# New half-step positions for projections, values, bulk loads and the last feed-forward stage in a two-layer gated cross-attention kernel

## The chip, the cores and the metric

The kernel runs on one core of one Trainium2 chip. The metric is the device time of one execution in microseconds (us). Engines are named as in the profile: PE is TensorE (matmul), DVE is VectorE, ACT is ScalarE, POOL is GpSimd, and SP is SyncE, whose queue issues nearly all DMA transfers. Each engine works through its own instructions in order and waits on semaphores for the others.

## What is computed

The input `x` has 4 sequences of 512 tokens with 256 features. Two layers follow each other. Each adds a gated cross-attention to `x`, and then a gated feed-forward part. The first layer's feed-forward part is a mixture of 8 experts, of which each token uses 2. The second layer's is two linear layers with ternary weights and 8-bit activations, with a gelu between them.

```
x = x + tanh(g_xattn[0]) * attention0(layernorm(x), ctx, ctx)
x = x + tanh(g_ffn[0])   * top2_experts(layernorm(x))
x = x + tanh(g_xattn[1]) * attention1(layernorm(x), ctx, ctx)
x = x + tanh(g_ffn[1])   * bitlinear(gelu(bitlinear(layernorm(x), w1)), w2)

attention: q, k, v = projections; 16 heads of 16 features
  softmax(q @ k.T / 4) @ v, then an output projection
```

## The kernel before, in words

**Phases and half steps.** There are 8 phases, one for each layer and sequence: phases 0 to 3 are the attention of layer 0, phases 4 to 7 that of layer 1. A phase has 16 groups of four heads by 128 keys, and each group is done in two halves, so that a phase has 32 half steps, called slots here (0 to 31). In each slot PE does two score matmuls `S` into the three banks of `psS` (L747), which DVE reduces to row maxima (L1166). It then does two transposed score matmuls `T` into `psT` (L761), which ACT turns into exponentials with one instruction of 128x1024 (L986). `S` runs 12 slots ahead of `T`, because the maxima have to be written back as extra rows of the queries first: POOL splits them in two parts (L643, L646), PE transposes them (L784), ACT copies them to `mt` (L1002), and SP writes them with four DMAs into `qs` (L526). In every odd slot PE also multiplies the exponentials of an earlier group with the values, `PV` (L775, eight matmuls in the trace). Every eighth slot (2, 10, 18, 26) has four transpositions of the attention's output, `NT` (L792), and every eighth (4, 12, 20, 28) one of the maxima, `MT` (L784).

**The other work.** All else is hung into slots by a table written by hand, `work_table`. `put(p, s, item)` puts an item behind the `S`, `T` and `PV` of slot `s` of phase `p`. `pair` puts an item for both halves of the features. Every engine walks through the same table and does its part of each item in that order. The items that matter here are:

- `SPLIT` (`K` or `Q`, phase, half): a projection, on PE four matmuls of 128x512 in the trace (L702) into a bank of `psX`. ACT then reads the bank twice (L933, L934), POOL forms the low part (L569), and SP writes both parts to DRAM (L498 to L502). They come back into `qs` and `ks` with `RELOAD` (L516).
- `VV`: the values, eight matmuls (L722) into `psX`, read by DVE (L1120).
- `LD`: bulk loads by SP (L444): `w1` and `w2` are 1 MB each into `hh`, `x3` 512 KB, `k1` 256 KB. `ABS` (L1131) and `QUANT` (L1151, L1154) are DVE's sums and ternary weights from `w1` and `w2`.
- `LNC` and `LNN`: the normalisation, eight small POOL operations (L586 to L605) and ACT's scaling (L943). `ST` is its statistics on DVE (L1095), `XT` the transposition (L733) with ACT's copy (L956), `BIAS` an addition on POOL (L616), `MH` a copy of expert weights on ACT (L971).
- In phases 5 to 7, and behind the last phase for the last sequence: `XQ`, `XI`, `XB` (scaling on POOL L652, rounding on ACT L1016, transposition L851 and ACT's copy L1026), `F1` (the first linear layer, L874, and ACT's gelu L1037 over 128x1024), `HQ` (DVE L1328 to L1338, POOL L658), `HS` (ACT L1048), `HT` (PE L884, ACT L1062), `F2` (PE L892, DVE L1348), `XOUT` (the output, SP L533). There are four tiles of 128 tokens each.

**Banks.** The small results share the two banks of `psX` in turn, and an item waits until the one before it in the same bank has been read. The gelu inputs `F1` of tiles 0 and 2 are written to the two banks of `psT`, those of tiles 1 and 3 to both banks of `psX`. ACT needs another function table for gelu than for the exponential, so the trace has a table load on either side of a block of gelus.

**Start and end.** The 12 slots ahead of phase 0 are slots 20 to 31 of a phase named `lead`, in which only `S` runs. In front of them the first two sequences are normalised and projected.

The functions of the kernel that the change touches are these.

## Time and profile before

| | before |
|---|---|
| device time, three runs | 811.45 us median (808.52 to 812.57) |
| profiled execution, its device time | 810.76 us |
| its span in the trace | 809.0 us |
| mean granted TensorE clock | 0.919 of full |
| busy PE, DVE, ACT, POOL | 709.5, 529.0, 448.7, 168.1 us |

The device time of the profiled execution is 1.8 us above its span. Slot starts are read off the exponentials (L986), of which there is one in each slot: the first starts at 53.5 us, the last phase's last one at 759.1 us. The phases start at 53.5, 145.1, 239.2, 328.5, 417.3, 506.2, 600.8 and 685.5 us, and slots 8 and 16 of phase 0 at 76.9 and 99.6 us.

### The profile page before, as it was taken

To read this page: it belongs to the slowest core of one execution; us is meant where nothing else is said; L and a number is where in the kernel's file an instruction comes from. 1 tells how busy PE (TensorE), PEld (TensorE's weight loads), DVE (VectorE), ACT (ScalarE), POOL (GpSimd) and SP (SyncE) were. 2 spreads that over 40 slices of the span, in tenths; PEclk is the share of its full clock that TensorE was granted. 3 is DMA by queue.
4 is the path that set the end of the run, shared out by engine and by line. 5 is a ranking of instruction groups with operands and counts; after the bars stand their busy time and mean duration, and the time that the engine had idled before them with its cause. 6 is when DMAs were issued, how large, how long until landed. Compare 5 with 4: busy or idle time off the path is not lost.

```text
span 809.0 us, 10145 instructions
## 1 busy us (share of the span) xinstructions
PE 709.5 (88%) x3554; PEld 333.6 (41%) x3554; DVE 529.0 (65%) x1138; ACT 448.7 (55%) x572; POOL 168.1 (21%) x302
## 2 busy tenths in 40 slices
...
DMA packets 39922, 66.74 MB, mean 82 GB/s; under 512 B 6080, under 2 KB 14784, under 8 KB 39616
## 3 DMA queue, kind: packets, MB, share of 16 engines
...
## 4 chain that ended last, share of the span: by engine, by line
PE 64%; ACT 12%; DVE 11%; issue 6%; POOL 5%; DMA 1%; SPq 0%; POOLq 0%; DVEq 0%; ACTq 0%
PE psO L775 14%; PE psS L747 7%; PE psT L761 7%; PE psX L702 7%; PE psX L836 5%; ACT pt L986 5%; DVE mx L1166 4%; PE psX L812 4%; PE psX L837 4%; PE psX L838 3%; PE psX L722 3%; PE psX L892 2%; DVE xs L1297 2%; PE psX L733 2%; ACT parts L934 1%
## 5 line engine op out<-in xcount | busy, mean ns | idle before, releaser
L1166 DVE TENSOR_REDUCE mx<-psS 128x1 f32<-128x512 f32 x512 | 324.7, 681 | 121.6 <-PE psS L747 121.3
L986 ACT ACTIVATE pt<-psT 128x1024 f32<-128x1024 f32 x256 | 261.6, 1022 | 225.1 <-PE psT L761 222.8
L747 PE MATMUL psS<-ks,qs 48*128 48x512 f32 x512 | 155.4, 519 | 16.6 <-DVE mx L1166 16.0
L775 PE MATMUL psO<-pt,vg 128*32 128x512 f32 x1024 | 148.6, 655 | 0.1
L761 PE MATMUL psT<-qs,ks 50*128 50x512 f32 x512 | 120.6, 444 | 24.1 <-ACT pt L986 22.2
L747 PEld LDWEIGHTS psS<-ks,qs 48*128 48x128 f32 x512 | 61.1, 194 | 128.2 <-issue 70.6
L1297 DVE SCALAR_TENSOR_TENSOR xs<-psX,coef,xs 128x256 f32<-128x256 f32 x128 | 61.8, 483 | 32.3 <-PE psX L838 29.2
L569 POOL TENSOR_TENSOR parts<-qf,parts 128x512 fp32r<-128x512 f32 x32 | 40.8, 1274 | 190.8 <-ACT parts L934 190.8
L761 PEld LDWEIGHTS psT<-qs,ks 50*128 50x128 f32 x512 | 53.3, 196 | 46.8 <-ACT pt L986 44.2
L836 PE MATMUL psX<-moeh,xh 128*128 128x512 f32 x128 | 57.5, 449 | 4.4 <-DVE xs L1297 4.4
L837 PE MATMUL psX<-moel,xh 128*128 128x512 f32 x128 | 51.0, 398 | 0.0
L838 PE MATMUL psX<-moeh,xl 128*128 128x512 f32 x128 | 50.3, 393 | 0.0
L702 PE MATMUL psX<-ctxb,wk 128*128 128x512 f32 x64 | 39.6, 754 | 7.6 <-DMA wk<-in_Wk 7.6
L836 PEld LDWEIGHTS psX<-moeh,xh 128*128 128x128 f32 x128 | 24.1, 189 | 43.6 <-DVE xs L1297 22.5
L643 POOL CAST mp<-mx 128x16 fp32r<-128x16 f32 x32 | 6.7, 208 | 169.6 <-DVE mx L1166 169.3
L943 ACT ACTIVATE xn<-xs,lnw 128x256 f32<-128x256 f32 x60 | 31.8, 590 | 15.8 <-POOL lnw L605 15.7
L658 POOL TENSOR_SCALAR hh<-hh,am 128x1024 f32<-128x1024 f32 x16 | 17.9, 1120 | 107.1 <-DVE am L1338 107.1
L775 PEld LDWEIGHTS psO<-pt,vg 128*32 128x32 f32 x1024 | 20.6, 110 | 43.3 <-issue 42.2
L702 PE MATMUL psX<-xnt,wq 128*128 128x512 f32 x64 | 35.0, 676 | 2.0 <-ACT xnt L956 1.6
L722 PE MATMUL psX<-wv,ctxb 128*128 128x256 f32 x128 | 32.8, 402 | 0.0
L812 PE MATMUL psX<-wo,ont 128*128 128x256 f32 x128 | 31.6, 391 | 0.8 <-ACT ont L979 0.8
L1095 DVE BATCH_NORM_STATS2 st<-xs 128x6 f32<-128x256 f32 x64 | 26.4, 413 | 7.3 <-DMA xs<-in_x 6.6
(128 smaller groups left out, 745.9 us busy)
## 6 DMA issues: line engine op xcount, KB each, us to landing
ks<-kd SPq DMA_DIRECT2D x64, 192.0 KB, 3.7
qs<-qd SPq DMA_DIRECT2D x64, 192.0 KB, 4.6
kd<-parts SPq DMA_DIRECT2D x16, 512.0 KB, 2.8
qd<-parts SPq DMA_DIRECT2D x16, 512.0 KB, 2.7
...
ctxb<-in_ctxT SPq DMA_DIRECT2D x7, 512.0 KB, 3.4
xs<-in_x SPq DMA_DIRECT2D x4, 512.0 KB, 6.8
```

The lines of the kernel that those rows point to most:

```text
L702: i = mm(o, w[:, k, c * P:(c + 1) * P], src[:, k, :], start=k == 0, stop=k == NC - 1)
L722: i = mm(o[:, t * D:(t + 1) * D], ctxb[:, p % 2, k, (2 * half + t) * P:(2 * half + t + 1) * P], wv[l][:, k, :], start=k == 0, stop=k == NC ...
L747: mm(psS[:, i % 3, :], qs[at:at + KR, 2 * g + a, k * P:(k + 1) * P], ks[at:at + KR, 2 * g + a, :], start=True, stop=True).then_inc(pe_s, 1)
L761: i = mm(psT[:, r, :], ks[at:at + KR + MP, 2 * g + half, k * P:(k + 1) * P], qs[at:at + KR + MP, 2 * g + half, :], start=True, stop=True)
L775: i = mm(psO[32 * j:32 * j + 32, :], vg[:, p % 2, k, g * GH + j, :], pt[:, s % RING, j, :], start=k == 0, stop=k == NT - 1, tile_position= ...
L812: i = mm(o[:, t * D:(t + 1) * D], ont[:, k, tt * P:(tt + 1) * P], wo[l][:, k, :], start=k == 0, stop=k == NC - 1)
L836: mm(o, xh[:, k, tok], moeh[:, k, at], start=k == 0, stop=False)
L837: mm(o, xh[:, k, tok], moel[:, k, at], start=False, stop=False)
L838: i = mm(o, xl[:, k, tok], moeh[:, k, at], start=False, stop=k == NC - 1)
L986: a(pt[:, G % RING, 2 * half:2 * half + 2, :], psT[:], ACT.Exp, scale=SCALE).then_inc(a_exp, 1)
L1166: v.tensor_reduce(mx[:, w // GH % 2, r, col:col + 1], psS[:, i % 3, :], AX.X, ALU.max).then_inc(v_max, 1)
L1297: v.scalar_tensor_tensor(out=xs[:, b, t, :], in0=o[:, k * D:(k + 1) * D], scalar=coef[:, t, e:e + 1], in1=xs[:, b, t, :], op0=ALU.mult, op ...
```

## The change

Nothing that is computed changes. The items have other places, `F1` of tiles 1 and 3 has other banks, and the waits follow the banks.

- The two projections `Q` of phase 1, until now ahead of the first exponential, stand in slots 0 and 4 of phase 0. All projections of phases 0 and 1 stand in even slots (14 in phase 0, where there were 10, and 2 in phase 1, where there were 4). In phases 5 and 6 the two `K` projections move from slots 1 and 13 to 2 and 12.
- The values of phase 1 move from slots 13 and 15 of phase 0 to 8 and 14.
- The loads `x3`, `w1`, `w2` and `k1` are issued in slots 0, 1, 3 and 4 of phase 0. They stood ahead of the first exponential.
- `ABS` moves from slots 3 and 5 to 9 and 11, the `QUANT` items to the even slots 14 to 28.
- `F1` of tiles 1 and 3 goes to the first two banks of `psS`. It waits for the maxima, and the next `S` waits for the gelus. In phases 5 and 6 the values stand behind `F1` of tiles 1 and 2; they stood ahead of tiles 0 and 1.
- Behind the last phase all four `F1` are done first, then all `HQ`, then `HS`, `HT` and `F2` in turn.

```diff
-    put(lead, 26, ("LD", ("w1",)))
-    put(lead, 28, ("LD", ("w2",)))
-    put(lead, 29, ("SPLIT", ("Q", 1, 1)))
...
-    pair(0, 23, "SPLIT", "K", 4, step=2)
-    pair(0, 27, "SPLIT", "K", 5, step=2)
...
+    put(0, 0, ("SPLIT", ("Q", 1, 0)), ("LD", ("x3",)), ("BIAS", (1, 0)))
+    put(0, 1, ("LD", ("w1",)))
...
+    pair(0, 20, "SPLIT", "K", 4, step=2)
+    pair(0, 24, "SPLIT", "K", 5, step=2)
...
-                put(p, 1, ("SPLIT", ("K", p + 1, 0)))
-                put(p, 13, ("SPLIT", ("K", p + 1, 1)))
+                put(p, 2, ("SPLIT", ("K", p + 1, 0)))
+                put(p, 12, ("SPLIT", ("K", p + 1, 1)))
...
-                if p < NP - 1 and t < 2:
-                    put(p, 16, ("VV", (p + 1, t)))
                 put(p, 16, ("F1", (t,)))
+                if p < NP - 1 and t in (1, 2):
+                    put(p, 16, ("VV", (p + 1, t - 1)))
...
-    out += [("LD", (one,)) for one in ("bo", "x2", "k1", "x3")]
+    out += [("LD", (one,)) for one in ("bo", "x2")]
...
-    out += [("SPLIT", ("Q", 1, 0))]
...
(scores S)
+                    if due(a_f1, n("F1")):
+                        pe.wait_ge(a_f1, n("F1"))
                     mm(psS[:, i % 3, :], qs[at:at + KR, 2 * g + a, k * P:(k + 1) * P], ks[at:at + KR, 2 * g + a, :],
...
(gelu input F1)
                 if t % 2:
-                    for b in range(2):
-                        if due(*last[b]):
-                            pe.wait_ge(*last[b])
-                        last[b] = (a_f1, i + 1)
-                    o = psX
+                    if due(v_max, n("S", 2)):
+                        pe.wait_ge(v_max, n("S", 2))
+                    o = psS
                 else:
                     if due(a_exp, n("T")):
                         pe.wait_ge(a_exp, n("T"))
-                    if due(a_f1, i - 1):
-                        pe.wait_ge(a_f1, i - 1)
                     o = psT
+                if due(a_f1, i - 1):
+                    pe.wait_ge(a_f1, i - 1)
                 if due(a_xb, n("XB")):
                     pe.wait_ge(a_xb, n("XB"))
```

Three places on PE show what the table does. The first is PE's order from the transposition of the second normalised sequence (L733, after the change L738) to the first exponentials' scores. `psS` are the scores for the maxima, `psT` the transposed ones, `mp` the maxima, and `psX<-xnt,wq` a projection of queries. Before:

```order
L733 MATMUL psX<-identf,xn 128x128 x8
L702 MATMUL psX<-xnt,wq 128x512 x2
L747 MATMUL psS<-ks,qs 128x512 x18
L784 MATMUL psX<-identf,mp 32x128
L747 MATMUL psS<-ks,qs 128x512 x2
L702 MATMUL psX<-xnt,wq 128x512 x2
L747 MATMUL psS<-ks,qs 128x512 x6
L761 MATMUL psT<-qs,ks 128x512 x2
L747 MATMUL psS<-ks,qs 128x512 x2
```

After:

```order
L738 MATMUL psX<-identf,xn 128x128 x8
L754 MATMUL psS<-ks,qs 128x512 x18
L791 MATMUL psX<-identf,mp 32x128
L754 MATMUL psS<-ks,qs 128x512 x8
L768 MATMUL psT<-qs,ks 128x512 x2
L707 MATMUL psX<-xnt,wq 128x512 x2
L754 MATMUL psS<-ks,qs 128x512 x2
```

The two projections have left the stretch ahead of the first `psT`; the first of them now stands right behind it.

The second place is PE in slots 24 to 28 of phase 0, where the projections of keys for later phases stand (`psX<-ctxb,wk`). `psO` is `PV`, and `identf,osb` is `NT`. Before:

```order
L747 MATMUL psS<-ks,qs 128x512 x2
L761 MATMUL psT<-qs,ks 128x512 x2
L747 MATMUL psS<-ks,qs 128x512 x2
L761 MATMUL psT<-qs,ks 128x512 x2
L775 MATMUL psO<-pt,vg 32x512 x4
L702 MATMUL psX<-ctxb,wk 128x512 x2
L747 MATMUL psS<-ks,qs 128x512 x2
L761 MATMUL psT<-qs,ks 128x512 x2
L792 MATMUL psX<-identf,osb 128x128 x4
```

After:

```order
L754 MATMUL psS<-ks,qs 128x512 x2
L768 MATMUL psT<-qs,ks 128x512 x2
L707 MATMUL psX<-ctxb,wk 128x512 x2
L754 MATMUL psS<-ks,qs 128x512 x2
L768 MATMUL psT<-qs,ks 128x512 x2
L782 MATMUL psO<-pt,vg 32x512 x4
L754 MATMUL psS<-ks,qs 128x512 x2
L768 MATMUL psT<-qs,ks 128x512 x2
L799 MATMUL psX<-identf,osb 128x128 x4
L707 MATMUL psX<-ctxb,wk 128x512 x2
```

The projection stood behind `PV` in the odd slot; it now stands directly behind `T` of the even slot, and in one even slot of four behind `NT`.

The third place is PE behind the last phase. `w1q,xit` is `F1`, `identb,hq` is `HT`, `w2q,hqt` is `F2`, and `identb,xi` is `XB`. Before:

```order
L851 MATMUL psX<-identb,xi 128x128 x4
L874 MATMUL psT<-w1q,xit 128x512 x4
L874 MATMUL psX<-w1q,xit 128x512 x4
L851 MATMUL psX<-identb,xi 128x128 x4
L874 MATMUL psT<-w1q,xit 128x512 x4
L884 MATMUL psX<-identb,hq 128x128 x8
L874 MATMUL psX<-w1q,xit 128x512 x4
L892 MATMUL psX<-w2q,hqt 128x256 x8
L884 MATMUL psX<-identb,hq 128x128 x8
L892 MATMUL psX<-w2q,hqt 128x256 x8
L884 MATMUL psX<-identb,hq 128x128 x8
```

After:

```order
L858 MATMUL psX<-identb,xi 128x128 x4
L879 MATMUL psT<-w1q,xit 128x512 x4
L858 MATMUL psX<-identb,xi 128x128 x4
L879 MATMUL psS<-w1q,xit 128x512 x4
L879 MATMUL psT<-w1q,xit 128x512 x4
L879 MATMUL psS<-w1q,xit 128x512 x4
L889 MATMUL psX<-identb,hq 128x128 x16
L897 MATMUL psX<-w2q,hqt 128x256 x8
L889 MATMUL psX<-identb,hq 128x128 x8
```

The fourth `F1` stood behind the first `HT`, which needs the first tile's whole way through `HQ` and `HS`; all four now stand together ahead of it.

## Rows read from the trace of the kernel before

**Rows 1.** The page: shares of the chain that ended last, by engine.
```profile
PE 64%; ACT 12%; DVE 11%; issue 6%; POOL 5%; DMA 1%; SPq 0%; POOLq 0%; DVEq 0%; ACTq 0%
```

**Rows 2.** Windows: stretch, us, PE, PEld, DVE, ACT, POOL busy, PEclk, DMA, GB/s.
```profile
0.00:53.50 53.50, 38.01 (x87) 17.68 (x87) 24.03 (x50) 13.72 (x23) 25.32 (x40) 0.81 0.87 256
53.50:76.90 23.40, 19.78 (x70) 6.75 (x69) 15.51 (x26) 13.12 (x19) 7.87 (x14) 0.71 0.47 167
...
99.60:145.10 45.50, 39.65 (x171) 14.98 (x170) 28.41 (x50) 26.97 (x37) 12.21 (x11) 0.92 0.49 151
...
761.20:809.00 47.80, 23.82 (x120) 14.14 (x116) 16.01 (x46) 20.53 (x25) 10.53 (x24) 0.70 0.03 11
```

**Rows 3.** Timeline ahead of the first exponential: start, us, engine, instruction, idle before.
```profile
29.12 3.75 PE L702 MATMUL psX<-xnt,wq 128*128 128x512 f32 x4 [0.78 <-ACT xnt L956]
...
32.80 0.93 PE L747 MATMUL psS<-ks,qs 48*128 48x512 f32 x3
...
45.07 2.84 SPq L526 DMA_DIRECT2D qs<-mt  x4
...
45.40 3.78 PE L702 MATMUL psX<-xnt,wq 128*128 128x512 f32 x4
...
52.97 0.50 PE L761 MATMUL psT<-qs,ks 50*128 50x512 f32 x2 [0.59 <-DMA qs<-mt]
```

**Rows 4.** DMA issues, median us to landing: 25:26.8 us, then 150:400 us.
```profile
qs<-qd SPq DMA_DIRECT2D x2, 192.0 KB, 3.7
...
kd<-parts SPq DMA_DIRECT2D x4, 512.0 KB, 2.8
```

**Rows 5.** Timeline of slots 23 to 25 of phase 0.
```profile
120.64 1.02 ACT L986 ACTIVATE pt<-psT 128x1024 f32<-128x1024 f32 x1 [0.60 <-PE psT L761]
...
121.52 1.98 PE L702 MATMUL psX<-ctxb,wk 128*128 128x512 f32 x4
...
124.70 1.02 ACT L986 ACTIVATE pt<-psT 128x1024 f32<-128x1024 f32 x1
...
126.31 1.02 ACT L986 ACTIVATE pt<-psT 128x1024 f32<-128x1024 f32 x1 [0.59 <-PE psT L761]
```

**Rows 6.** A group of DVE: `ABS`; busy us, mean ns, idle before.
```profile
L1131 DVE TENSOR_REDUCE wsum<-hh 128x1 f32<-128x2048 f32 x2 | 4.5, 2264 | 0.0
```

**Rows 7.** Timeline of slots 16 and 17 of phase 1.
```profile
191.34 1.98 PE L702 MATMUL psX<-ctxb,wk 128*128 128x512 f32 x4
...
191.45 1.02 ACT L986 ACTIVATE pt<-psT 128x1024 f32<-128x1024 f32 x1 [4.08 <-PE psT L761]
...
194.51 1.02 ACT L986 ACTIVATE pt<-psT 128x1024 f32<-128x1024 f32 x1
```

**Rows 8.** Timeline of slots 13 and 14 of phase 6.
```profile
631.74 1.02 ACT L986 ACTIVATE pt<-psT 128x1024 f32<-128x1024 f32 x1 [0.74 <-PE psT L761]
...
638.46 1.02 ACT L986 ACTIVATE pt<-psT 128x1024 f32<-128x1024 f32 x1
```

**Rows 9.** Timeline of slot 16 of phase 5: second gelu and next exponential.
```profile
562.18 1.11 ACT L1037 ACTIVATE hh<-psX,am 128x1024 f32<-128x1024 f32 x1 [2.51 <-PE psX L874]
...
566.85 1.02 ACT L986 ACTIVATE pt<-psT 128x1024 f32<-128x1024 f32 x1
```

**Rows 10.** Timeline behind the last phase.
```profile
781.21 1.11 ACT L1037 ACTIVATE hh<-psX,am 128x1024 f32<-128x1024 f32 x1 [0.35 <-PE psX L874]
...
784.15 1.88 PE L874 MATMUL psT<-w1q,xit 128*128 128x512 bf16 x4 [0.69 <-ACT xit L1026]
...
792.35 1.11 ACT L1037 ACTIVATE hh<-psX,am 128x1024 f32<-128x1024 f32 x1 [1.98 <-PE psX L874]
...
806.38 0.48 DVE L1348 SCALAR_TENSOR_TENSOR xs<-psX,am,xs 128x256 f32<-128x256 f32 x1 [2.61 <-PE psX L892]
```

**Rows 11.** Groups in 778:809 us: busy us, mean ns, idle before.
```profile
L1048 ACT ACTIVATE hq<-hh,negm 128x1024 bf16<-128x1024 f32 x4 | 4.6, 1138 | 0.0
L1062 ACT ACTIVATE hqt<-psX 128x1024 bf16<-128x1024 bf16 x4 | 4.1, 1023 | 6.7 <-PE psX L884 6.7
```

More of the change, by code:

```diff
@@ L111, in work_table @@
-    put(0, 5, ("LNN", (2, 0, 2)), ("SPLIT", ("K", 1, 1)), ("ABS", (1,)))
-    put(0, 6, ("LNN", (2, 2, 4)))
-    pair(0, 7, "XT")
-    put(0, 8, ("BIAS", (2, 0)))
-    put(0, 9, ("SPLIT", ("Q", 2, 0)), ("LD", ("moe1",)))
-    put(0, 10, ("WS", ()))
-    put(0, 11, ("SPLIT", ("Q", 2, 1)))
-    put(0, 13, ("VV", (1, 0)), ("LNC", (3, 0, NT)))
-    put(0, 15, ("VV", (1, 1)), ("LNN", (3, 0, 2)))
-    put(0, 16, ("LNN", (3, 2, 4)))
-    pair(0, 17, "XT")
-    put(0, 18, ("BIAS", (3, 0)))
-    pair(0, 19, "SPLIT", "Q", 3, step=2)
@@ L124, in work_table @@
-    pair(0, 23, "SPLIT", "K", 4, step=2)
-    put(0, 22, ("LD", ("v1",)))
-    put(0, 26, ("LD", ("q1",)), ("CTX", (2,)))
-    pair(0, 27, "SPLIT", "K", 5, step=2)
-    put(0, 30, ("CTX", (3,)))
-    for q, s in enumerate((11, 13, 15, 19, 21, 23, 25, 27)):
-        put(0, s, ("QUANT", (q // 4, q % 4)))
-    pair(1, 1, "SPLIT", "K", 2, step=3)
-    pair(1, 6, "SPLIT", "K", 3, step=10)
+        st(0, 5 + t, 3, t)
+    put(0, 0, ("SPLIT", ("Q", 1, 0)), ("LD", ("x3",)), ("BIAS", (1, 0)))
+    put(0, 1, ("LD", ("w1",)))
@@ new lines, in work_table @@
+    put(0, 2, ("SPLIT", ("K", 1, 0)))
+    put(0, 3, ("LNC", (2, 0, NT)), ("LD", ("w2",)))
+    put(0, 4, ("SPLIT", ("Q", 1, 1)), ("LD", ("k1",)))
+    put(0, 5, ("LNN", (2, 0, 2)))
+    put(0, 6, ("SPLIT", ("K", 1, 1)), ("LNN", (2, 2, 4)))
+    pair(0, 7, "XT", step=2)
+    put(0, 8, ("VV", (1, 0)), ("BIAS", (2, 0)), ("LD", ("moe0",)))
+    put(0, 9, ("ABS", (0,)), ("LNC", (3, 0, NT)))
+    pair(0, 10, "SPLIT", "Q", 2, step=2)
+    put(0, 11, ("ABS", (1,)), ("LNN", (3, 0, 2)))
+    put(0, 12, ("LNN", (3, 2, 4)), ("LD", ("moe1",)))
@@ new lines, in work_table @@
+    pair(0, 13, "XT", step=2)
+    put(0, 13, ("WS", ()))
+    put(0, 14, ("VV", (1, 1)), ("BIAS", (3, 0)))
+    pair(0, 16, "SPLIT", "Q", 3, step=2)
+    put(0, 18, ("LD", ("o",)))
+    pair(0, 20, "SPLIT", "K", 4, step=2)
+    put(0, 23, ("CTX", (2,)))
+    pair(0, 24, "SPLIT", "K", 5, step=2)
+    put(0, 25, ("LD", ("rt",)))
+    put(0, 27, ("CTX", (3,)))
+    pair(0, 28, "SPLIT", "K", 2, step=2)
+    put(0, 29, ("LD", ("v1",)))
+    for q in range(8):
+        put(0, 14 + 2 * q, ("QUANT", (q // 4, q % 4)))
@@ L133, in work_table @@
+    pair(1, 0, "SPLIT", "K", 3, step=2)
+    put(1, 4, ("LD", ("q1",)))
     for i in range(MOE_PARTS):
```

25 lines of the change are left out of this document (13 added, 12 removed).

## The prediction

> **What bounds the kernel now.** I read the shares of the chain first, then the windows by stage, then the timelines of the places that the change touches. PE has 64% of the chain that ended last [rows 1], but that is a mean over stages. The windows [rows 2] tell four of them apart. Ahead of the first exponential (53.5 us) PE is granted 0.81 of its clock and the DMA engines are busy at 0.87. The first 8 slots of phase 0 take 23.4 us at a granted clock of 0.71. Slots 16 to 31 take 45.5 us at 0.92. The last 47.8 us have PE busy for half of the time, at 0.70.
>
> Inside phase 0 the chain goes back and forth. An exponential starts, PE does `PV` and then the projection, ACT has to read the projection twice, and the next exponential stands behind those reads. In slot 23 the exponential starts at 120.64, the projection only at 121.52, and the next exponential at 124.70: 4.06 us [rows 5]. The even slot behind it, with no projection, takes 126.31 - 124.70 = 1.61 us. Of the 4.06 us, 0.88 is `PV`, which nobody awaits so soon. So what counts is what stands between `T` and ACT's reads. That is what the change touches.
>
> **Start: -5.5 us.** A projection of 3.75 us (29.12 to 32.8) stands ahead of the first `S` at 32.80 [rows 3]. Without it `S` waits for `qs`, whose two writes are issued from 25 us on and land 3.7 us later [rows 4], so at about 29.5: 3.3 us earlier. The way from there to the DMAs of the maxima (45.07) keeps its length, 12.3 us, since DVE's maxima set it. They start at 41.8 instead of 45.07, and the last of the four is issued 2.1 us later, at 43.9. Before, `T` waited for them until 52.97, 5 us behind the last issue, with `w1` in the queue ahead of them. With the bulk loads gone I take the 2.8 us of a write in a calm stretch [rows 4], which gives 46.7. Ten maxima between are DVE's at some 0.6 us each, 41.8 - 1 + 6.2 = 47.0. The second projection (45.40, 3.78 us at the low clock) is gone as well. So `T` starts near 47.3 instead of 52.97; I take -5.5. The bounds are -3.3 (the landing stays as it was) and -6.2.
>
> The trace shows the maxima's writes landing only behind `w1`. The Trainium skill states as a rule that each DMA engine takes the descriptors of one issuing engine's ring in order (DMA: Bandwidth & Descriptors, section on queues, rings and completion order), and by that rule the trace agrees. By it the wait isn't lost but moved: the bulk now stands ahead of phase 0's own transfers. That is the second rival below.
>
> **Phases 0 and 1: -6 us.** The price of a projection is what its slot takes above 1.61 us. In an odd slot that is 4.06 - 1.61 = 2.45 us [rows 5]. For an even slot there is one at full clock before: slot 16 of phase 1, 191.45 to 194.51, 3.06 us, with the projection starting at 191.34, right at the exponential [rows 7]. Its price is 1.45 us. `PV` then falls into the next slot, beneath ACT's reads and the exponential.
> - Before: 10 odd in phase 0, 1 odd and 3 even in phase 1: 11 x 2.45 + 3 x 1.45 = 31.3 us. After: 16 even, 23.2 us. This has the two `Q` that come out of the start in it. -8.1 us.
> - In slots 0 to 7 (clock 0.71) two projections ran at the low clock, at 3.78 instead of 1.98 us [rows 3, 5]. I expect one to stay so, the one in slot 0, and the denser PE to be granted the full clock behind it: -1.8 us.
> - The two `VV` no longer stand behind `PV`: 2 x 0.88 = -1.8 us.
> - Against it: `NT` stands ahead of a projection in slots 10, 18 and 26, `MT` in 4, 12, 20 and 28. Both are shorter than `PV`'s 0.88; I take 0.5 and 0.3, together +2.7 us.
> - `ABS` blocks DVE for 2.26 us twice [rows 6]. In slots 3 and 5 that lay beside slow projections; in 9 and 11 there is none, and two of DVE's maxima per slot are late. `S` has three banks, so a part is absorbed: +1.5 us each, +3 us.
> - POOL (1.3 us a projection), SP and the DMAs have a pair of slots, 4.7 us, for each: hidden.
>
> The sum is -6.0. Its bounds are +2 (an even slot is worth nothing, `NT`, `MT` and `ABS` cost in full, the clock gives nothing) and -11 (they cost nothing).
>
> **Phases 5 and 6: -8 us.** `K` from slot 1 to 2: 1.0 us each, -2. `K` from 13 to 12: slot 13 of phase 6 takes 638.46 - 631.74 = 6.72 us [rows 8], with `PV` and the projection at the low clock. In slot 12 the projection runs on PE beneath ACT's four scalings (slot 11) and the exponential, so that only ACT's two reads remain. The bounds are 0 and -3.8; I take -2 each, -4. In phase 5 POOL did the low part of the slot 1 projection ahead of the normalisation of slot 1, for which ACT waits in slot 3: -1. The gelus: in phase 5 ACT sat 2.51 us ahead of the second [rows 9], since `F1` of tile 1 waited for `VV` in `psX`. But both `VV` now stand between tile 1 and tile 3, and PE's work in the block stays 6.9 us, so most of the gap comes back ahead of the third and fourth: I take -0.6 each, -1.2 (bounds 0 and -2.5 each).
>
> The block has a new wait: `S` of slot 17 waits for the fourth gelu, and behind it on PE stand `T` and `PV`; ACT's next exponential waits for `T`. ACT loads its table meanwhile (the exponential at 566.85 [rows 9] is 1.3 us behind the last gelu), and `S` plus `T` need 0.8 us at full clock, so it costs nothing; at the low clock it would cost 0.3 us.
>
> **End: -8 us.** Before, the second gelu starts at 781.21, then ACT turns to `XI` and `XB` of the second half, PE's third `F1` follows at 784.15, and the fourth gelu starts at 792.35, behind `HS` and `HT` of tile 0 [rows 10]. After, `XI` is done ahead of the first gelu and `XB`'s copy behind it, at 781.5. `F1` of tile 1 waits for that copy, which isn't needed for its tile: gelu 1 at 782.4 (full clock, half of the 1.88 us) or 783.3, so 1 to 2 us later than before. The others follow at 1.05 us or, at the low clock, at 1.7 us. The fourth ends at 785.8 to 787.8 instead of 793.5. Then ACT has 4 `HS` of 1.14 and 4 `HT` copies of 1.02 [rows 11], 8.6 us. The last `HS` waits for DVE's and POOL's part of tile 3, which is due near 790.5 and ready in time. The last transposition (1.0), the last `F2` (1.0 to 1.9) and DVE's 0.48 come behind: 796.9 to 800.6. Before, the last DVE operation ends at 806.86 [rows 10]. So -6.3 to -10; I take -8.
>
> **Sum.** -5.5 - 6 - 8.2 - 8 = -27.7. The profiled execution took 810.76 us, of which 809.0 are its span; that gives 783.1. The median of the runs shown is 0.7 us above the profiled one. I predict 783 us.
>
> **Rivals.**
> - *PE is the bound and the half step doesn't matter.* For it: 64% of the chain, and PE's total work is unchanged. Against it: 3.06 against 4.06 us in the rows. Then phases 0, 1, 5 and 6 keep their length and only start and end remain: 810.8 - 13.5 = 797 us. Chance 0.13.
> - *The bulk stands in the way of phase 0.* `x3`, `w1` and `w2` (2.5 MB) and two projections' parts (1.5 MB) are issued ahead of the second group's maxima (slot 4), which are due for `T` in slot 8. 4.0 MB at the start's 256 GB/s [rows 2] are 16 us from about 54, so 70, against slot 8 near 70 to 72. A few us of wait there, some at `ST` of `x3` (DVE's maxima queue behind it) and at later reloads make +8: 791 us. Chance 0.15. This is what the ring order of the Trainium skill's DMA page would do here.
> - *The clock stays low: slower.* With a projection in every second slot at the low clock, a pair of slots has 8.7 us of PE work instead of 4.7: the projection +1.8 [rows 3, 5], and as much again for scores and `PV`, so +4 us a pair. Seven such pairs of the 16 in phase 0 eat the 28 us, eight make it 815. For it: slots 0 to 7 had 0.71. Against it: slots 16 to 31 had 0.92 with the same work less dense. Chance 0.03. The Trainium skill (TensorE: Matmul & The Clock Gate, part on the HAM clock gate) has it that idleness lowers the clock and activity releases it, which speaks against this rival.
>
> **Numbers.** The forecast has 0.69, with a range of its own of 775 to 791. The range for all is 773 to 797: below it are the far bounds of start, slots and end together, above it half of the first rival and the third. About 0.5% is what a measurement can tell here. Faster by more: 0.95; within: 0.02; slower: 0.03.
>
> **What would show it.** First exponential near 48 us. Slots 20 to 31 of phase 0 in pairs of 3.1 and 1.6 us. Phases 2, 3 and 4 at 89 us as before. Slots 12 to 15 of phases 5 and 6 shorter by 2 us. Four gelus without a gap behind the last phase and the fourth ending by 788. I am wrong if the even slots take 4 us, if `T` of slot 8 waits for `mt`, or if PE's clock in phase 0 is under 0.8.

## The result, and the profile after

The changed kernel takes 768.44 us (median of 4 runs, 766.51 to 770.32) against 809.99 us before (4 runs, 806.96 to 812.57). The ratio is 0.9488, with a 95% interval of 0.9442 to 0.9534. I had predicted 783.0 us with a range of 773 to 797: the direction was right, the gain of 41.5 us is one and a half times the forecast one of 27.7, and the time lies below the range. A ratio leaves out the runs that lie more than 1.5% above the fastest run of their kernel.

The profiled execution has a span of 764.7 us against 809.0. Cut at the first exponential of each phase, and for the end where the last exponential stops (760.2 us before, 724.9 after; [rows 2] cuts at 761.2), the windows are these (us, busy us of PE, PEld, DVE, ACT, POOL with instructions, PEclk, DMA share, GB/s), for the start, phases 0, 1, 5, 6 and 7, and the end:

```profile
0.00:46.90 46.90, 30.68 (x78) 15.62 (x78) 23.62 (x50) 11.06 (x19) 21.08 (x37) 0.81 0.76 216
46.90:132.10 85.20, 78.39 (x355) 30.30 (x356) 63.15 (x112) 56.98 (x80) 31.13 (x41) 0.97 0.71 231
132.10:222.10 90.00, 84.27 (x439) 42.19 (x440) 65.80 (x150) 47.08 (x64) 19.29 (x28) 0.98 0.28 72
488.60:572.40 83.80, 75.00 (x434) 34.32 (x435) 59.51 (x119) 62.04 (x77) 20.14 (x37) 0.98 0.29 84
572.40:650.50 78.10, 68.47 (x412) 31.57 (x412) 57.07 (x114) 56.80 (x67) 12.93 (x26) 1.00 0.26 69
650.50:724.90 74.40, 62.59 (x358) 25.79 (x358) 41.19 (x87) 54.35 (x61) 10.05 (x22) 0.91 0.07 17
724.90:764.70 39.80, 22.15 (x123) 13.46 (x124) 15.92 (x46) 20.34 (x26) 10.58 (x24) 0.79 0.05 16
```

The kernel before, cut in the same way, for phases 5 and 6:

```profile
506.20:600.80 94.60, 84.10 (x435) 36.72 (x435) 59.70 (x119) 62.40 (x77) 20.07 (x37) 0.87 0.27 74
600.80:685.50 84.70, 74.59 (x413) 32.83 (x412) 57.32 (x114) 57.04 (x67) 12.95 (x26) 0.92 0.24 64
```

The reader is to compare PE in phase 5: 435 matmuls before and 434 after, but 84.10 us busy before and 75.00 after, at a granted clock of 0.87 and 0.98. Phases 5 and 6 together lose 15.2 us of PE's busy time with the same work. The clock has two levels here, 2.4 GHz (granted 1.0) and 1.2 GHz (0.5), so a window of 94.60 us at 0.87 holds 2 x 0.13 x 94.6 = 25 us at the low one. Read from the clock's own records it is 23.9 us. By stage (us of length, and behind the stroke the us of it at 1.2 GHz; 2 to 4 are three phases together, of some 89 us each):

| | start | 0 | 1 | 2 to 4 | 5 | 6 | 7 | end | span |
|---|---|---|---|---|---|---|---|---|---|
| before | 53.5/21 | 91.5/21 | 94.1/7 | 267.0/3 | 94.6/24 | 84.7/14 | 74.7/14 | 48.8/28 | 809.0 |
| after | 46.9/18 | 85.1/6 | 90.0/3 | 266.6/0 | 83.8/3 | 78.1/0 | 74.4/14 | 39.8/17 | 764.7 |
| difference | -6.6 | -6.4 | -4.1 | -0.5 | -10.8 | -6.6 | -0.3 | -9.0 | -44.3 |
| predicted | -5.5 | -6, both | | 0 | -8.2, both | | 0 | -8 | -27.7 |

The whole program had 131 us at the low clock before and 61 us after. These are one execution of each kernel, but the sign isn't luck: of the 33 runs of before beside the experiments none has a mean granted clock above 0.937, and of the 8 runs of the changed kernel none has one below 0.953. The chain that ended last has changed with it; to [rows 1] answers:

```profile
PE 56%; DVE 14%; ACT 12%; issue 9%; POOL 6%; DMA 2%; SPq 0%; POOLq 0%; DVEq 0%; ACTq 0%
```

**Start.** The timeline of after, up to the first exponential, which answers to [rows 3] (start, us, engine, instruction, idle before and who ended it):

```profile
29.61 1.22 PE L754 MATMUL psS<-ks,qs 48*128 48x512 f32 x3 [2.11 <-DMA qs<-qd]
...
42.03 2.84 SPq L531 DMA_DIRECT2D qs<-mt  x4
...
46.06 0.80 PE L768 MATMUL psT<-qs,ks 50*128 50x512 f32 x2
46.79 1.22 PE L707 MATMUL psX<-xnt,wq 128*128 128x512 f32 x1
46.90 1.02 ACT L991 ACTIVATE pt<-psT 128x1024 f32<-128x1024 f32 x1 [4.90 <-PE psT L768]
```

`S` starts at 29.61 where I had said 29.5, the four writes are issued at 42.03 (41.8), and `T` at 46.06 no longer waits for them: its line has no bracket.

**Phase 0.** Slots 24 and 25 of after, with a projection in the even one. This answers to [rows 5] and [rows 7]:

```profile
111.94 1.98 PE L707 MATMUL psX<-ctxb,wk 128*128 128x512 f32 x4
112.05 1.02 ACT L991 ACTIVATE pt<-psT 128x1024 f32<-128x1024 f32 x1 [0.69 <-PE psT L768]
...
113.96 0.69 ACT L938 ACTIVATE qf<-psX,bkc 128x512 f32<-128x512 f32 x1 [0.89 <-PE psX L707]
...
114.55 0.68 ACT L939 ACTIVATE parts<-psX,bkc 128x512 fp32r<-128x512 f32 x1
115.12 1.02 ACT L991 ACTIVATE pt<-psT 128x1024 f32<-128x1024 f32 x1
...
116.73 1.02 ACT L991 ACTIVATE pt<-psT 128x1024 f32<-128x1024 f32 x1
```

The even slot takes 115.12 - 112.05 = 3.07 us, the odd one 1.61: the pair takes 4.68 where it took 5.67 before.

**Phase 6.** Slots 12 and 13 of after, beside [rows 8]:

```profile
599.50 1.88 PE L707 MATMUL psX<-ctxb,wk 128*128 128x512 f32 x4
600.63 1.00 ACT L991 ACTIVATE pt<-psT 128x1024 f32<-128x1024 f32 x1
...
602.83 1.00 ACT L991 ACTIVATE pt<-psT 128x1024 f32<-128x1024 f32 x1
...
604.42 1.03 ACT L991 ACTIVATE pt<-psT 128x1024 f32<-128x1024 f32 x1 [0.59 <-PE psT L768]
```

The projection lies beneath ACT's scalings and the exponential, and takes 1.88 us instead of 3.78. Slots 12 and 13 take 2.2 and 1.6 us, where they took 1.9 and 6.7.

**End.** The timeline of after from the rounding of the second half (L1021) to the fourth gelu (L1042), which answers to [rows 10]:

```profile
740.45 0.72 ACT L1021 ACTIVATE xi<-xn,negm 128x512 bf16<-128x512 f32 x1
...
743.00 1.49 PE L879 MATMUL psT<-w1q,xit 128*128 128x512 bf16 x3 [1.09 <-ACT xit L1031]
...
744.52 1.11 ACT L1042 ACTIVATE hh<-psT,am 128x1024 f32<-128x1024 f32 x1 [0.81 <-PE psT L879]
745.53 0.59 ACT L1031 ACTIVATE xit<-psX 128x512 bf16<-128x512 bf16 x1
...
746.27 1.86 PE L879 MATMUL psS<-w1q,xit 128*128 128x512 bf16 x4 [1.36 <-ACT xit L1031]
...
748.17 1.11 ACT L1042 ACTIVATE hh<-psS,am 128x1024 f32<-128x1024 f32 x1 [2.05 <-PE psS L879]
...
750.52 1.11 ACT L1042 ACTIVATE hh<-psS,am 128x1024 f32<-128x1024 f32 x1
```

The fourth gelu ends 26.7 us behind the last exponential (724.9); it was 33.3 us before. The second gelu still waits 2.05 us, for an `F1` that waited for the second half's copy and then ran at the low clock.

### The profile page after: what moved, and what is told of

Its sections match the earlier page's. It is cut to its first block, busy times and chain, and to the rows that moved or that the text cites. A ratio compares the mean times of both kernels' runs of the same rounds, so it can differ in the third digit from the quotient of the medians.

```text
span 764.7 us, 10140 instructions
## 1 busy us (share of the span) xinstructions
PE 676.7 (88%) x3550; PEld 323.6 (42%) x3554; DVE 530.5 (69%) x1138; ACT 446.8 (58%) x572; POOL 167.0 (22%) x302
## 4 chain that ended last, share of the span: by engine, by line
PE 56%; DVE 14%; ACT 12%; issue 9%; POOL 6%; DMA 2%; SPq 0%; POOLq 0%; DVEq 0%; ACTq 0%
PE psO L782 10%; PE psS L754 7%; PE psX L707 7%; DVE mx L1171 6%; PE psT L768 6%; PE psX L843 5%; PE psX L819 4%; ACT pt L991 4%; PE psX L844 4%; PE psX L845 4%; PE psX L727 3%; ACT qf L938 2%; DVE xs L1302 2%; POOL parts L574 2%; ACT parts L939 2%
## 5 line engine op out<-in xcount | busy, mean ns | idle before, releaser
L1171 DVE TENSOR_REDUCE mx<-psS 128x1 f32<-128x512 f32 x512 | 325.1, 681 | 87.4 <-PE psS L754 86.1
L754 PE MATMUL psS<-ks,qs 48*128 48x512 f32 x512 | 153.8, 516 | 18.9 <-DVE mx L1171 13.2
L782 PE MATMUL psO<-pt,vg 128*32 128x512 f32 x1024 | 140.4, 621 | 0.1
L768 PE MATMUL psT<-qs,ks 50*128 50x512 f32 x512 | 118.2, 431 | 9.6 <-ACT pt L991 8.2
L843 PEld LDWEIGHTS psX<-moeh,xh 128*128 128x128 f32 x128 | 23.9, 187 | 43.9 <-DVE xs L1302 23.8
L707 PE MATMUL psX<-ctxb,wk 128*128 128x512 f32 x64 | 34.4, 667 | 7.7 <-DMA wk<-in_Wk 7.7
L707 PE MATMUL psX<-xnt,wq 128*128 128x512 f32 x64 | 32.2, 630 | 1.3 <-ACT xnt L961 0.8
L1125 DVE TENSOR_TENSOR vg<-psX,bvb 128x512 f32<-128x512 f32 x16 | 11.0, 691 | 29.1 <-PE psX L727 29.1
```

What stands on the lines that cost most here:

```text
L707: i = mm(o, w[:, k, c * P:(c + 1) * P], src[:, k, :], start=k == 0, stop=k == NC - 1)
L754: mm(psS[:, i % 3, :], qs[at:at + KR, 2 * g + a, k * P:(k + 1) * P], ks[at:at + KR, 2 * g + a, :], start=True, stop=True).then_inc(pe_s, 1)
L768: i = mm(psT[:, r, :], ks[at:at + KR + MP, 2 * g + half, k * P:(k + 1) * P], qs[at:at + KR + MP, 2 * g + half, :], start=True, stop=True)
L782: i = mm(psO[32 * j:32 * j + 32, :], vg[:, p % 2, k, g * GH + j, :], pt[:, s % RING, j, :], start=k == 0, stop=k == NT - 1, tile_position= ...
L843: mm(o, xh[:, k, tok], moeh[:, k, at], start=k == 0, stop=False)
L1171: v.tensor_reduce(mx[:, w // GH % 2, r, col:col + 1], psS[:, i % 3, :], AX.X, ALU.max).then_inc(v_max, 1)
```

## The experiments

Each took its place beside runs of the kernel before on the same chip. x1 to x4 shared one chip (before: 807.75 us, median of 7), y1 to y3 and z1 another (807.6, 19 runs), the last four a third (802.62, 7 runs). Lengths of stages are those of each kernel's profiled execution. The intervals of the ratios reach 0.4 to 1.2% to either side, so the lengths of the stages, and not the whole times, tell the theories apart.

**x1_k56: only the projections of phases 5 and 6, in the kernel before.**

```diff
-                put(p, 1, ("SPLIT", ("K", p + 1, 0)))
-                put(p, 13, ("SPLIT", ("K", p + 1, 1)))
+                put(p, 2, ("SPLIT", ("K", p + 1, 0)))
+                put(p, 12, ("SPLIT", ("K", p + 1, 1)))
```

> The kernel before with one part of the change: in phases 5 and 6 the two key projections stand in slots 2 and 12 instead of 1 and 13. Theory CLOCK (the low-clock stretches of phases 5 and 6, 23.9 and 13.7 us of them before and 3.4 and 0 after, came from PE standing idle ahead of the projections, and go with the move): phases 5 and 6 shorten together by 12 us or more, their granted clock rises from 0.87 and 0.92 to over 0.96, ratio near 0.98. Theory PRICE (only the slots that hold the projections get shorter, as the prediction had it): 6 to 7 us, low-clock time nearly as before, ratio near 0.992.

Measured: 797.21 us, ratio 0.987 (0.9782 to 0.9959), 10.5 us less than before. Phase 5 takes 87.9 us (-6.7) and phase 6 78.8 (-5.9). The windows:

```profile
503.10:591.00 87.90, 79.73 (x436) 35.34 (x435) 59.74 (x120) 62.04 (x76) 20.06 (x37) 0.92 0.28 82
591.00:669.80 78.80, 70.08 (x413) 31.41 (x412) 57.13 (x113) 56.80 (x66) 12.88 (x26) 0.98 0.26 68
```

With two lines moved by one slot the two phases are 12.6 us shorter, against the 7 us that I had for them. Of the 12.6, 2.4 are slot 5 of phase 5, which is shorter in x2_end too, without this edit. PE's busy time in the two falls by 8.9 us with the same instructions, as the granted clock goes from 0.87 and 0.92 to 0.92 and 0.98. Slots 12 to 15 take 10.7 and 8.4 us instead of 12.7 each. Neither theory was met in full: the 12 us of CLOCK came, but the granted clock of phase 5 stayed at 0.92 (10.2 us at the low clock from 559.7 us on), and the ratio lies between the two that were named.

**x2_end: only the gelus' banks, the values between them and the order of the end, in the kernel before.**

```diff
-                if p < NP - 1 and t < 2:
-                    put(p, 16, ("VV", (p + 1, t)))
                 put(p, 16, ("F1", (t,)))
+                if p < NP - 1 and t in (1, 2):
+                    put(p, 16, ("VV", (p + 1, t - 1)))
...
+    put(NP, 5, ("F1", (0,)), ("XB", (2, 4)), ("F1", (1,)), ("F1", (2,)), ("F1", (3,)))
...
-                a(hh[:, t, :], (psX if t % 2 else psT)[:].rearrange("p a b -> p (a b)"), ACT.Gelu,
+                a(hh[:, t, :], (psS if t % 2 else psT)[:, 0:2, :].rearrange("p a b -> p (a b)"), ACT.Gelu,
```

> The kernel before with the new banks for the gelu inputs, the values behind the inputs of tiles 1 and 2, and the new order of the end. Both theories: the end takes 7 to 9 us less; slot 16 of phases 5 and 6 0.2 to 0.6 us less each; phases 0 to 4 unchanged. CLOCK adds that phases 5 and 6 keep their low-clock stretches ahead of slot 16, so that no more than 2 us come from them: ratio near 0.988.

Measured: 795.88 us, ratio 0.988 (0.9783 to 0.9977), with runs from 784 to 809 us, of which the profiled one is the fastest. The end takes 40.1 us, 8.7 less than before. Slot 16 of phases 5 and 6 goes from 11.1 and 10.8 to 10.6 us, and slots 17 to 21 of phase 5 from 13.3 to 10.2. In x1_k56, which left the block alone, these take 13.3 as before. So the gelus themselves gave 0.6 us, and the slots behind them 3.1 in phase 5, where before had 10.2 us at the low clock from 569.2 on and this kernel has none. Slots 12 to 15 stayed at 12.7 and 13.4 us, so what was gained there belongs to `K`. What was gained behind slot 16 goes with the block's new order, but it is the low clock that went and not work that got shorter. In the eight cases with the old order (phases 5 and 6 of before, x1_k56, y1_fill6 and y3_lnc) slots 17 to 21 take between 13.3 us, with 10.2 at the low clock, and 9.5 us, with none. The new order takes 10.2 in every profile, with no low clock, and at the full clock the old one is the shorter of the two.

Two parts of the expectation missed. Phases 5 and 6 are 6.6 us shorter, not 2 at most. And phases 0 and 1, where this kernel has the same instructions as before, took 88.2 and 91.0 us instead of 91.5 and 94.1, with 13 us at the low clock instead of 27. One execution of the same instructions differs from another by 6.4 us there.

**x3_odd: the projections and values of phases 0 and 1 one slot later, in the changed kernel.**

```diff
-    pair(0, 16, "SPLIT", "Q", 3, step=2)
-    pair(0, 20, "SPLIT", "K", 4, step=2)
-    pair(0, 24, "SPLIT", "K", 5, step=2)
+    pair(0, 17, "SPLIT", "Q", 3, step=2)
+    pair(0, 21, "SPLIT", "K", 4, step=2)
+    pair(0, 25, "SPLIT", "K", 5, step=2)
...
```

> The changed kernel with the 16 projections and the 2 values of phases 0 and 1 one slot later, in the odd slots, all else as changed. Theory PRICE: 16 projections at 1.0 us and 2 values at 0.9 us more, less some 2 us because the transpositions of the attention output and of the maxima no longer stand ahead of them: phases 0 and 1 longer by 14 to 16 us. Rival (PE is the bound in these phases, the half step doesn't matter, and the gain there came from the clock and from moving the sums of the weights): longer by less than 5 us.

Measured: 791.62 us, ratio 0.974 (0.9623 to 0.9858). Phases 0 and 1 take 107.3 and 92.2 us, together 24.3 more than in the changed kernel and more than the 14 to 16 expected. The window of phase 0:

```profile
47.00:154.30 107.30, 92.15 (x356) 35.13 (x355) 65.36 (x112) 57.29 (x80) 27.75 (x39) 0.88 0.57 180
```

In slots 16 to 31 the pairs stand at 4.1 + 1.6 us again. With the one disturbed slot (25, 5.7 us) counted at 4.1, these sixteen take 45.5 us against 39.9, 0.7 us for each of the eight projections; the prediction had 1.0, less 0.17 for `NT` and `MT`. That gives 11 us for 16. Of the 24.3, 7.1 lie in slots 16 to 31, 2.2 in phase 1 and 15.0 in slots 0 to 15, 60.2 us against 45.2, with 23 us at the low clock there instead of 6. The half step has nearly its forecast price where the clock is full, and more time at the low clock goes with it. How much of the 15.0 us is the one and how much the other this run can't tell, since the sums of the weights on DVE (L1136) stand beside projections here.

**x4_loads: the bulk loads back ahead of the first exponential, in the changed kernel.**

```diff
+    put(lead, 26, ("LD", ("w1",)))
+    put(lead, 28, ("LD", ("w2",)))
...
-    put(0, 1, ("LD", ("w1",)))
```

`w2`, `k1` and `x3` go back in the same way.

> The changed kernel with the four bulk loads back ahead of the first exponential, the projections staying in phase 0. If the wait of the first T for the maxima's writes came from the loads ahead of them in the queue, the first exponential is later by 3 to 5 us and phase 0 keeps its length. Rival (the 6.5 us of the start came from the two projections alone): first exponential later by less than 1 us. If the bulk costs phase 0 something in the changed kernel, phase 0 gets shorter here by what it costs; I expect less than 1.5 us.

Measured: 772.43 us, ratio 0.9579 (0.9503 to 0.9654). The start takes 50.6 us (+3.7), phase 0 86.1 (+1.0). The timeline:

```profile
38.01 0.43 SPq L450 DMA_DIRECT2D hh<-in_w  x1
...
41.90 2.84 SPq L532 DMA_DIRECT2D qs<-mt  x4
...
44.78 0.44 SPq L450 DMA_DIRECT2D hh<-in_w  x1
...
49.81 0.80 PE L769 MATMUL psT<-qs,ks 50*128 50x512 f32 x2 [3.55 <-DMA qs<-mt]
```

The first `hh<-in_w` is `w1`, issued ahead of the maxima's writes, and the second is `w2`, issued behind them. The chain that ended last has the fourth write from its issue to its landing:

```profile
44.10 5.66 DMA qs<-mt
```

`T` waits 3.55 us for the writes of the maxima again. `w1` took 10.9 us to land, to 48.9, and the fourth write landed at 49.8, ahead of `w2` (7.1 us, to 51.9): the load that stood ahead of the writes held them up. Of the 6.6 us at the start, 3.7 are the loads' and the other 2.9 the two projections'. Phase 0 isn't shorter for having its loads done early, so the bulk was not in its way. One reservation: the start scatters too, 46.7 to 47.1 us in six other profiles with the changed start and 49.7 in z2_q12, where `T` doesn't wait for the writes.

**y1_fill6: five matmuls that nobody reads behind slot 11 and five behind slot 12, in phases 5 and 6, in the kernel before.** Nothing else is moved, and nothing is left out.

```diff
+    for p in (5, 6):
+        put(p, 11, ("FILL", (5,)))
+        put(p, 12, ("FILL", (5,)))
...
+                for _ in range(count):
+                    mm(psX[:, b, :], identb[:], w1q[:, 0, 0:S], start=True, stop=True)
```

> The kernel before with ten idle matmuls of 128x512 in each of phases 5 and 6 (five in slot 11, five in slot 12, their result is never read), nothing moved. They add 2.2 us of PE work per phase at full clock, in a stretch in which PE stands idle. Theory CLOCK: the low clock that comes in slots 12 and 13 (6.8 us of it in phase 6, the projection at 3.78 us) is gone or shorter, and slots 12 to 15 of phases 5 and 6, 12.6 us each before, shrink to about 11 although work was added. Theory PRICE (it is the order of the work alone): they stay at 12.6 us or grow by up to 2.2.

Measured: 800.11 us (10 runs), ratio 0.9921 (0.9876 to 0.9965). Work was added and the kernel got 0.8% faster. Phase 5 takes 88.9 us (-5.7), phase 6 82.0 (-2.7); slots 12 to 15 take 9.9 and 10.1 us instead of 12.7 each, with no low clock. In phase 6 slots 10 and 11 grew by 0.9 us, with 3.4 us at the low clock from 620.2 us on. Slot 13 of phase 6, with the added matmuls (L905) ahead of it:

```profile
624.93 1.24 PE L905 MATMUL psX<-w1q,identb 128*128 128x512 bf16 x5
...
626.89 1.02 ACT L998 ACTIVATE pt<-psT 128x1024 f32<-128x1024 f32 x1 [0.80 <-PE psT L765]
627.77 1.99 PE L706 MATMUL psX<-ctxb,wk 128*128 128x512 f32 x4
...
629.79 0.69 ACT L945 ACTIVATE qf<-psX,bkc 128x512 f32<-128x512 f32 x1 [1.88 <-PE psX L706]
...
630.95 1.02 ACT L998 ACTIVATE pt<-psT 128x1024 f32<-128x1024 f32 x1
```

The slot takes 4.06 us, as any odd slot at full clock, instead of 6.72: the projection 1.99 instead of 3.78. The kernel before has PE waiting ahead of this slot, and the slow projection in it:

```profile
630.90 0.79 PE L761 MATMUL psT<-qs,ks 50*128 50x512 f32 x2 [1.59 <-ACT pt L986]
...
633.48 3.78 PE L702 MATMUL psX<-ctxb,wk 128*128 128x512 f32 x4
```

It waited 1.59 us, behind ACT's four scalings, and the low clock began at 630.6, within that wait. With PE kept busy it didn't. This isn't one lucky execution: with `K` in slot 13 and nothing added, slots 12 to 15 have 5.9 to 9.5 us at the low clock in all six cases (phases 5 and 6 of before, x2_end and y3_lnc), and none in the two of y1_fill6. The Trainium skill (TensorE: Matmul & The Clock Gate, part on the HAM clock gate) says that idleness drops the clock and activity raises it; this pair of runs agrees, 3.78 against 1.99 us.

**y3_lnc: the normalisation ahead of the projection in slot 1 of phase 5 alone, in the kernel before.**

```diff
-                put(p, 1, ("SPLIT", ("K", p + 1, 0)))
+                if p != B + 1:
+                    put(p, 1, ("SPLIT", ("K", p + 1, 0)))
...
             put(p, 1, ("LNC", (p - 2, 0, NT)))
+            if p == B + 1:
+                put(p, 1, ("SPLIT", ("K", p + 1, 0)))
```

> The kernel before with one thing in phase 5: the normalisation's small POOL operations of slot 1 stand ahead of the projection of slot 1 instead of behind it, so that POOL doesn't do the projection's low part first. PRICE: slot 3 of phase 5 falls from 4.2 to about 3.0 us, nothing else: -1.2 us. CLOCK: PE's idle stretch ahead of the low clock of slots 3 to 5 goes, slot 5 falls from 4.0 to 1.6 us as well: phase 5 shorter by 3 us or more.

Measured: 799.0 us (10 runs), ratio 0.9919 (0.9871 to 0.9967). Phase 5 takes 88.8 us (-5.8). Slot 3 of phase 5, before:

```profile
514.09 1.02 ACT L986 ACTIVATE pt<-psT 128x1024 f32<-128x1024 f32 x1 [0.60 <-PE psT L761]
...
516.85 1.09 ACT L943 ACTIVATE xn<-xs,lnw 128x256 f32<-128x256 f32 x2 [1.75 <-POOL lnw L605]
...
518.33 1.01 ACT L986 ACTIVATE pt<-psT 128x1024 f32<-128x1024 f32 x1
```

and in y3_lnc:

```profile
507.56 1.02 ACT L989 ACTIVATE pt<-psT 128x1024 f32<-128x1024 f32 x1 [0.60 <-PE psT L764]
...
508.48 1.08 ACT L946 ACTIVATE xn<-xs,lnw 128x256 f32<-128x256 f32 x2
...
509.94 1.02 ACT L989 ACTIVATE pt<-psT 128x1024 f32<-128x1024 f32 x1
```

ACT's wait of 1.75 us for POOL is gone and the slot takes 2.38 instead of 4.24 us. Slot 5 went from 4.0 to 1.6 as well: before, 6.8 us at the low clock began at 518.0, right behind that wait. But slot 5 takes 1.6 in x2_end too, where slot 3 is as before (4.3). So the 2.4 us of slot 5 can't be given to this edit by these runs. Nor can the last 1.5 us of phase 5, or the 3.4 and 3.0 us by which phases 0 and 1 are shorter here as they are in x2_end.

**y2_fill7: twelve such matmuls behind slots 11 and 12 of phase 7, in the changed kernel,** which still has 13.7 us at the low clock there.

```diff
+    put(7, 11, ("FILL", (5,)))
+    put(7, 12, ("FILL", (7,)))
```

> The changed kernel with twelve idle matmuls of 128x512 in phase 7 (five in slot 11, seven in slot 12; their result is never read), where no projection stands. Before and after the change this stretch has up to 13.7 us of low clock. CLOCK: no low clock in slots 11 to 15, which sum to 10.7 us for slots 12 to 15 before, and 8 to 9 now; the whole 0 to 2 us faster than the changed kernel. PRICE: slots 12 to 15 keep 10.7 us or grow.

Measured: 767.76 us, ratio 0.9509 (0.9409 to 0.961). Slots 12 to 15 of phase 7 take 8.5 us instead of 10.7, and the phase 73.2 instead of 74.4. But the changed kernel itself, profiled a second time (a_again, below), has 71.6 us there with nothing added. The run settles nothing: whether these slots fall at the low clock differs from one execution to the next.

**z1_tail: no needless wait and idle matmuls at the end, in the changed kernel.** `F1` of the first two tiles waits only for its own half's copy, 28 matmuls fill PE's idle time behind the output projection and 8 that behind the last `F1`.

```diff
+    put(NP, 4, ("FILL", (28,)))
...
+    put(NP, 5, ("FILL", (8,)))
...
-                if due(a_xb, n("XB")):
-                    pe.wait_ge(a_xb, n("XB"))
+                ready = n("XB") - (n("XB") == 5 and t < 2)
+                if due(a_xb, ready):
+                    pe.wait_ge(a_xb, ready)
```

> The changed kernel with two additions at the end: F1 of tile 1 no longer waits for the second XB copy (its tile doesn't use it), and PE does 28 idle matmuls of 128x512 behind the last output projection and 8 behind the last F1 (results never read), where it stands idle otherwise. CLOCK: the 17.1 us of low clock in the end become less than 7; F1, HT and F2 run at full clock; the end (39.8 us) takes 3.5 to 5 us less. PRICE alone: the freed wait gives 1.5 us, the idle matmuls nothing or a loss of 0 to 1 us.

Measured: 764.33 us, ratio 0.9483 (0.9383 to 0.9582). The end takes 36.3 us instead of 39.8, at the full clock throughout:

```profile
725.90:762.00 36.10, 25.02 (x158) 14.10 (x156) 15.84 (x46) 20.04 (x25) 10.54 (x24) 1.00 0.05 16
```

The four gelus start at 744.42, 745.95, 747.21 and 748.22, with the copy (0.58 us) behind the first and no wait over 0.15 us between them. The stage's 3.5 us is shown: the end takes 36.3 us in z4_both and z5_vv14 too, and 40.1 in a_again. How it divides between the freed wait and the idle matmuls isn't, since no run has one without the other. That the whole kernel got faster isn't: the changed kernel as it is had no run on that chip, and y2_fill7, which is near to it, had 767.76 us.

**a_again: the changed kernel once more,** beside the following three.

> The changed kernel once more, unaltered, as the base for the other three on the same chip. Expected: 766 to 771 us, and low-clock time of under 12 us in phases 0 to 6 together, as the first profile had it (12.5 us). If the clock's share in the gain was luck of one profile, the low-clock time is 30 us or more, or the time is above 775.

Measured: 767.3 us, ratio 0.9552 (0.9482 to 0.9621). The stages agree with the first profile within 1 us, but for phase 7 (71.6 against 74.4) and its 10 us less at the low clock. Phases 0 to 6 have 17 us at the low clock, more than the 12 expected and less than the 30 that would have meant luck. Against before on this chip the gain is 35.3 us, where it was 41.5 in the result; 767.3 us still lies below the range.

**z2_q12: the query projections of phases 2 to 5 in slots 10 and 12 instead of 9 and 10, in the changed kernel.**

```diff
-            pair(p, 9, "SPLIT", "Q", B + p - 2)
+            pair(p, 10, "SPLIT", "Q", B + p - 2, step=2)
```

> The changed kernel with the query projections of phases 2 to 5 in slots 10 and 12 instead of 9 and 10. PRICE: the one in slot 9 (4.1 us) leaves an odd slot with PV: 1.0 us less in each of 4 phases, -4 us. Rival (slots 7 to 11 are full of output projections and scalings, so that the moved projection only pushes the transposition of slot 12): -1 to +1 us.

Measured: 773.08 us, ratio 0.963 (0.9565 to 0.9696). This missed: slot 9 falls from 4.1 to 2.7 us, but slot 10 rises by 0.2 and slot 12 from 1.6 to 3.7, and phases 2 and 4, with no low clock in either, take 89.2 and 89.3 us instead of 88.9. Slot 12 already has the transposition of the normalised input and ACT's copy of it. An even slot isn't cheap by itself; it is cheap if ACT has nothing else there. The start was 2.6 us longer here (49.7): it is behind from the first projection of queries on, which begins at 17.8 us instead of 16.6 and runs at the low clock. What set that off in this execution isn't known.

**z4_both: z1_tail and z2_q12 together.** The edits are the two above.

> The two additions together: the query projections of phases 2 to 5 in slots 10 and 12, and at the end the freed wait of F1 and 36 idle matmuls that keep PE busy. If the parts add up: 3.5 us from the end and what the projections alone give, so some 7 us below the changed kernel on this chip, near 761 us.

Measured: 768.51 us, ratio 0.9561 (0.95 to 0.9622): less than hoped for, and no better than the changed kernel. The end keeps its 36.2 us, but phases 2 to 4 take 269.7 instead of 266.6: some 0.4 in each from the query projection, and 2 in phase 3, which has 6.8 us at the low clock here as in z2_q12.

**z5_vv14: z4_both with the second half of the values in slot 14 instead of 15, in phases 1 to 4.**

```diff
-                put(p, 15, ("VV", (p + 1, 1)))
+                put(p, 14, ("VV", (p + 1, 1)))
```

> As the one before, and the second values item of phases 1 to 4 in slot 14 instead of 15. PRICE: it leaves the odd slot with PV, 0.9 us less in each of 4 phases, -3.5 us. Rival (slot 14 holds the router's 16 small matmuls, so that the two add up there): 0 to -1 us.

Measured: 760.65 us (757.25 to 765.83), ratio 0.9482 (0.9412 to 0.9551), and 6.7 us below the changed kernel on the same chip: the fastest version of this study. Phases 2 to 4 take 88.4 us each. Slots 14, 15 and 16 of phase 2 take 3.8, 1.7 and 1.9 us instead of 2.2, 3.6 and 2.4, 0.8 less together, of which z2_q12's edit takes 0.4 back. Four phases at 0.8 are 3.3 us, near the 3.5 expected; the rest of the 7.9 us by which it is faster than z4_both isn't this edit's by the slots. Phase 3 has no low clock here, nor have phases 5 and 6. By stages the gain over a_again is 3.9 us at the end, 1.5 in phase 1, 1.4 in phases 2 to 4 and 1.6 in phase 5. The last goes with 3.4 us at the low clock that this execution doesn't have there. Whether z5_vv14 would be better still without z2_q12's edit was not run.

## Why the prediction was right or wrong

**Start, -5.5: right, measured -6.6.** The times on the way were met within 0.4 us up to the writes. `T` began 1.2 us ahead of the 47.3 of the forecast, since no wait for the landing shows there at all: PE went to it straight from its last `S`.

**Phases 0 and 1, -6: the mechanism was right, some sizes were off; measured -10.5, of which up to 6 belong to the execution of before.** The even slot takes 3.07 us and the odd one 1.61, as worked out, and x3_odd gives the half step its price. Slots 16 to 31 take 39.9 us. `ABS` was put at +3: slots 9 and 11, where it runs now, take 2.2 and 1.9 us in all, and nobody is recorded as waiting for its 2.28 us. That `psS`'s three banks absorb it is the likely reason. `MT` was put at 0.3: slots 20 and 28 take 0.6 more than slots 22 and 24. The clock was put at -1.8: the two phases had 27 us at the low clock before and 9 after. What the clock gave I can only bound: at 1.2 GHz work on PE takes about twice as long (3.78 against 1.98 us), so 18 us at the low clock fewer is at most 9 us. Part of that is no doing of the change. The phases have the same instructions in before, x1_k56, x2_end, y1_fill6 and y3_lnc, and took 185.6, 182.7, 179.2, 185.3 and 179.2 us together, with 27, 21, 13, 27 and 13 us at the low clock. In six profiles with the changed ones they took 174.9 to 178.6. Between the medians (182.7 and 175.6) the gain is 7.1 us, close to the forecast.

**Phases 5 and 6, -8.2: this is the step that failed; measured -17.4.** The prediction took the work of these phases at one clock, but for the projection in slot 13, and put the clock in them at nothing. By its terms, from the slots of the two profiles:

- `K` from slot 1 to 2 was put at -1.0 a phase. Slots 1 and 2 together went from 5.7 to 5.3 and 5.2 us: -0.4 each, and slot 3 of phase 6 gave another 0.5.
- `LNC` was put at -1. Slot 3 of phase 5 went from 4.24 to 2.37: -1.9, the whole wait for POOL (y3_lnc).
- `K` from 13 to 12 was put at -2 a phase. Slots 12 to 15 went from 12.7 to 10.0 in phase 5 and to 8.4 in phase 6: -7.0 in all. The bound of -3.8 was passed once. I had seen that the projection in the slot of [rows 8] ran at the low clock, and hid it beneath ACT's work, without asking what made the clock low: PE's idle time ahead of it, which the projection in slot 12 now fills. y1_fill6 shows that by itself: 5.4 us of these slots come from ten idle matmuls a phase, with the projection left in slot 13. It also gives the two parts in phase 6, where the changed kernel has no low clock in these slots: 12.7 to 10.1 us is the clock (-2.6, put at nothing), and 10.1 to 8.4 the place (-1.7, put at -2).
- The gelus were put at -1.2. Slot 16: -0.6.
- Nothing was put for the slots behind the block. Slots 17 to 21 gave -4.4 us (13.3 to 10.2 and 11.5 to 10.2), all of it by the clock: 17 us at 1.2 GHz before and none after. With the old order seven of eight cases have 3.4 to 10.2 us at the low clock there, with the new one none has any, so the order matters. That the values between the gelus keep PE busy is a likely cause, but no run moved them alone, and y1_fill6 takes most of it away with the old order.
- Nor for slot 5 of phase 5, -2.4. It lost the low clock of before. x2_end has the same instructions as before up to that slot and lost it too, so it can be a matter of the execution: whether the change did it isn't shown.

In the two phases the time at the low clock fell from 38 us to 3. The prediction counted the clock at the start of phase 0 and at the end. It had the place for it in phases 5 and 6 as well: slot 13 of phase 6 takes 6.72 us [rows 8], and the prediction says itself that the projection there ran at the low clock.

**End, -8: right, measured -9.0.** The fourth gelu was forecast 25.6 to 27.6 us behind the last exponential and ended at 26.7; the wait of `F1` for a copy that its tile doesn't use came as said, and z1_tail took it away. The sign of four gelus without a gap didn't come, because of that wait.

**Sum.** Of the 16.6 us by which the sum fell short of the two profiles, 9.2 are phases 5 and 6, 4.5 phases 0 and 1, 1.1 the start and 1.0 the end, and 0.8 the phases that the change doesn't touch. Between the medians of the runs it fell short by 13.8. By stage all the errors have one sign, and the largest have one cause, less time at the low clock. That is also why the range failed. With the far bounds of the start (-6.2), phases 0 and 1 (-11) and the end (-10), and phases 5 and 6 left at -8.2, the time is 775.4, close to the lower end of 773. The far bounds that the prediction gives for phases 5 and 6 itself add up to -15.6, which would have made it 768; that this is near the measured time is luck, since the 17.4 us came from other terms.

**Rivals.** That PE bounds the kernel and the half step doesn't matter fell with x3_odd (+24.3 us). That the bulk would stand in the way of phase 0 fell with x4_loads. That the clock would stay low fell with the granted clock of phase 0, 0.97.
